# A scan with an FFN woven in: loads of delta moved up in the queue's list, and ScalarE's takes from the shared PSUM bank moved behind tanh

## The reference, cut to what matters

```python
x = _layernorm(x + _L0_attn_ref(x, ...))
x = _layernorm(x + _L0_ffn_ref(x, W1, W2, W3))      # silu(x W1) * (x W3), fwht, W2
x = _layernorm(x + _L1_attn_ref(x, W_bc, W_dt, b_dt, A_log, D_param))
x = _layernorm(x + _L1_ffn_ref(x, w_gate_up, w_down))
...
# _L1_attn_ref: 2 sequences of 1024 tokens, 512 channels, 32 states each
delta = softplus(dt_r @ W_dt + b_dt)                # dt_r, Bm, Cm are parts of x @ W_bc
def step(h, inp):                                   # over the time of one sequence
    dA  = exp(delta_t[:, :, None] * A[None])
    dBu = (delta_t * u_t)[:, :, None] * B_t[:, None, :]
    h   = dA * h + dBu
    y_t = einsum('bdn,bn->bd', h, C_t)
```

## Time and profile before

| | |
|---|---|
| median of three runs | 1904.08 us (1896.26 to 1905.1) |
| profiled execution | 1897.86 us, span 1896.0 us |
| TensorE busy | 1761.6 us (93%), 9472 matmuls |
| VectorE busy | 1328.4 us (70%), 1532 instructions |
| GpSimd busy | 1285.5 us (68%) |
| ScalarE busy | 983.3 us (52%) |
| loads of delta | 256, 512 KB each, median 5.5 us to landing |

### The profile page before, as it was taken

How to read it: one execution, slowest core, us unless ns; L and a number is a source line. 1 busy time by engine, 2 the same in 40 slices (tenths; PEclk the granted TensorE clock), 3 DMA queues, 4 the chain that set the end, 5 groups by cost and what they waited for, 6 DMA issues and landing times. The chain is left out here.

```text
span 1896.0 us, 27444 instructions
## 1 busy us (share of the span) xinstructions
PE 1761.6 (93%) x9472; PEld 1152.8 (61%) x9472; DVE 1328.4 (70%) x1532; ACT 983.3 (52%) x1671; POOL 1285.5 (68%) x992
## 2 busy tenths in 40 slices
PE   7898998898998999989899899988999999999998
PEld 5566666576755565555555555555556555667886
DVE  2525344332259999799897999889999999994222
ACT  5344343566465656645566556556555655543212
POOL 4533445255449998688887998888889898883111
PEclk9999999999999999999999999999999999999999
DMA  7442332587668887678676887777678777874652
GB/s 244 129 144 74 123 105 97 184 304 269 242 215 277 290 297 254 211 265 289 226 252 230 291 283 257 230 243 248 230 264 280 253 258 260 278 265 157 209 191 97
DMA packets 159226, 427.32 MB, mean 225 GB/s; under 512 B 30992, under 2 KB 54096, under 8 KB 158704
## 3 DMA queue, kind: packets, MB, share of 16 engines
q1 hardware_dynamic: 159088, 425.57, 66.6%
HBM read 356.30 MB, written 69.21 MB: 224 GB/s over the span
## 5 line engine op out<-in xcount | busy, mean ns | idle before, releaser
L1630 ACT ACTIVATE decay<-delta_on_states,a_neg 128x512 f32<-128x512 f32 x512 | 354.2, 693 | 361.8 <-DVE h_states L1770 336.2
L1865 POOL TENSOR_TENSOR q_or_raw_or_h_times_c<-h_states,c_rep 128x512 f32<-128x512 f32 x293 | 382.0, 1316 | 63.9 <-PE scan_y L1464 34.3
L1865 POOL TENSOR_TENSOR h_times_c_rest<-h_states,c_rep 128x512 f32<-128x512 f32 x219 | 283.8, 1306 | 43.7 <-DVE h_states L1770 22.0
L1831 POOL TENSOR_TENSOR h_lo<-v_or_silu_in_h_lo,h_hi 128x512 fp32r<-128x512 f32 x128 | 167.9, 1312 | 205.4 <-ACT h_hi L1537 204.8
L1770 DVE TENSOR_TENSOR_SCAN h_states<-decay,h_last,d_b 128x512 f32<-128x512 f32 x192 | 243.2, 1281 | 9.2 <-ACT decay L1630 4.4
L1770 DVE TENSOR_TENSOR_SCAN h_states<-decay,d_b 128x512 f32<-128x512 f32 x192 | 231.4, 1216 | 14.8 <-ACT decay L1630 10.5
L111 PE MATMUL y_or_aux<-h_hi,w 128*128 128x512 f32 x468 | 208.2, 445 | 8.5 <-POOL h_lo L1831 5.2
L1455 PE MATMUL du_spread<-stack,selectors 96*128 96x512 bf16 x512 | 159.0, 389 | 48.8 <-DVE d_b L1739 22.5
L1696 DVE SCALAR_TENSOR_TENSOR v_or_silu_in_h_lo<-v_or_silu_in_h_lo,gate_or_scores 128x512 f32<-128x512 f32 x127 | 86.5, 681 | 147.7 <-ACT v_or_silu_in_h_lo L1533 147.3
L112 PE MATMUL y_or_aux<-h_lo,w 128*128 128x512 f32 x468 | 185.1, 395 | 0.0
L113 PE MATMUL y_or_aux<-h_hi,w 128*128 128x512 f32 x468 | 184.3, 394 | 0.0
(11 more groups left out here) (252 smaller groups left out, 4187.9 us busy)
## 6 DMA issues: line engine op xcount, KB each, us to landing
delta_on_states<-delta SPq DMA_DIRECT2D x256, 512.0 KB, 5.5
w<-w_split SPq DMA_DIRECT2D x112, 512.0 KB, 4.2
attn_w_hi_or_x_hi_w<-w_split SPq DMA_DIRECT2D x112, 512.0 KB, 4.1
attn_w_lo_or_x_lo_w<-w_split SPq DMA_DIRECT2D x112, 512.0 KB, 4.2
w_split<-w_presplit_hi_lo SPq DMA_DIRECT2D x32, 512.0 KB, 3.3
w_presplit_hi_lo<-in_w13b SPq DMA_DIRECT2D x32, 256.0 KB, 3.7
w_split<-attn_w_hi_or_x_hi_w SPq DMA_DIRECT2D x8, 1024.0 KB, 6.4
w_split<-attn_w_lo_or_x_lo_w SPq DMA_DIRECT2D x8, 1024.0 KB, 7.0
```

The lines of the kernel that those rows point to most:

```text
L1630: act.activation(da[:, s % ND], dring[:, s % NR], ACT.Exp, scale=a[:, column(s):column(s) + 1]).then_inc(s_da, 1)
L1831: pool.tensor_tensor(hl[:, idx % RH], sg[:, idx % RH], hh[:, idx % RH].bitcast(F32), ALU.subtract).then_inc(s_hl, 1)
L1865: pool.tensor_tensor(hc[s % NC_], hs[:, s % NH], crep[:, tile_of(s // SPO) % 2], ALU.mult).then_inc(s_hc, 1)
```

## The change

Three edits. `delta_load` stands first in SyncE's tick of an even step, for the pair s+6, where it stood late in the tick of the odd step behind it. `dt_take` stands one tick later for the tiles prepared in the scan (the matmul stays), and the last two tiles' `states` move by one tick, matmul and copy. In the scan's ticks the whole list of ScalarE's takes (`take_bank`) stands behind `tanh`, `h_high` and `copy_input`, not ahead of them. Ahead of the scan the order is as it was.

```diff
--- before.py
+++ after.py
@@ -955,7 +955,7 @@
 SPLIT_TICK = (FIRST_TICK, 84, 163, 282, 374, 469, 556, 665)
 RANK_TICK = (106, 215, 312, 408)
 DT_TICK = ((107, 109, 111, 112), (216, 221, 225, 229), (317, 321, 325, 329), (413, 417, 421, 425))
-STATES_TICK = ((114, 115), (233, 235), (330, 332), (426, 428))
+STATES_TICK = ((114, 115), (233, 235), (331, 333), (427, 429))
 SOFT_TICK = (((108, (0,)), (114, (1, 2, 3))), ((230, (0, 1, 2, 3)),), ((330, (0, 1, 2, 3)),), ((426, (0, 1, 2, 3)),))
 PARTS_TICK = ((109, 123, 131, 139), (231, 239, 247, 255), (332, 340, 348, 356), (428, 435, 442, 449))
 PARTS_STEPS = (0, 1, 2, 1, 3, 5, 6, 8)
@@ -997,6 +997,7 @@
 RANK_AT = at_tick(RANK_TICK)
 RANK_COPY_AT = {tick + (t > 0): t for t, tick in enumerate(RANK_TICK)}
 DT_AT = at_tick_by_m(DT_TICK)
+DT_TAKE_AT = {tick + (key[0] > 0): key for tick, key in DT_AT.items()}
 STATES_AT = at_tick_by_m(STATES_TICK)
 SIZE_AT, INPUT_AT, HIGH_AT, DELTA_STORE_AT, REST_AT, MID_AT, LOW_AT, PARTS_STORE_AT = (
     at_tick_by_m(PARTS_TICK, step) for step in range(8))
@@ -1290,6 +1291,8 @@
                 constants()
                 for tick in range(FIRST_TICK, LAST_TICK):
                     s = step_at(tick)
+                    if s >= 0 and s % 2 == 0 and s + NR < STEPS:
+                        delta_load((s + NR) // 2)
                     if tick in RAW13_AT:
                         raw13_load(RAW13_AT[tick])
                     if tick in W13_STORE_AT:
@@ -1315,8 +1318,6 @@
                     if s == -4:
                         for pair in range(NR // 2):
                             delta_load(pair)
-                    if s >= 0 and s % 2 == 1 and s + NR - 1 < STEPS:
-                        delta_load((s + NR - 1) // 2)
                     o, step = divmod(s, SPO)
                     if s >= 0 and step == 20 and 2 <= o + 1 < NO:
                         stack_load(o + 1)
@@ -1641,15 +1642,7 @@
                     act.wait_ge(s_hs, s + 2)
                     act.copy(last[:, column(s):column(s) + 2], hs[:, s % NH:s % NH + 2, TT - 1]).then_inc(s_ca, 1)
 
-                for tick in range(FIRST_TICK, LAST_TICK):
-                    s = step_at(tick)
-                    if tick in W13_HIGH_AT:
-                        w13_high(W13_HIGH_AT[tick])
-                    if s == -1:
-                        copy_input(0)
-                        copy_input(1)
-                    if 0 <= s + 1 < STEPS:
-                        decay(s + 1)
+                def take_bank(tick):
                     if tick in MEAN_PARTS_AT:
                         mean_parts(MEAN_PARTS_AT[tick])
                     if tick in MEAN_AT:
@@ -1662,14 +1655,28 @@
                         rank_copy(RANK_COPY_AT[tick])
                     if tick in STATES_AT:
                         states_copy(*STATES_AT[tick])
-                    if tick in DT_AT:
-                        dt_take(*DT_AT[tick])
+                    if tick in DT_TAKE_AT:
+                        dt_take(*DT_TAKE_AT[tick])
+
+                for tick in range(FIRST_TICK, LAST_TICK):
+                    s = step_at(tick)
+                    if tick in W13_HIGH_AT:
+                        w13_high(W13_HIGH_AT[tick])
+                    if s == -1:
+                        copy_input(0)
+                        copy_input(1)
+                    if 0 <= s + 1 < STEPS:
+                        decay(s + 1)
+                    if tick < SCAN_TICK:
+                        take_bank(tick)
                     if tick in TANH_AT and TANH_AT[tick]:
                         tanh(TANH_AT[tick])
                     if tick in H_SPLIT_AT:
                         h_high(H_SPLIT_AT[tick])
                     if 0 <= s < STEPS and s % JB == 1 and s // JB + 2 < STEPS // JB:
                         copy_input(s // JB + 2)
+                    if tick >= SCAN_TICK:
+                        take_bank(tick)
                     if s >= 4 and s % 2 == 0 and s - 4 < STEPS and keeps(s - 4):
                         carry(s - 4)
                     for e, k in SQUARE_AT.get(tick, ()):
```

## The result

The changed kernel takes 1905.15 us in the median of 21 runs, the kernel before 1897.43 us on the same chip: ratio 1.0049, 95% interval 1.0037 to 1.0061. It is slower, by about 9.3 us (0.0049 x 1897). The whole interval lies over 1, where I had forecast no change; the difference is just inside my bound of 0.5%, and 1905.15 is inside the range, but the sum of the parts gave +1.8 us, and the difference is five times that. That 1905.15 is close to the 1905.9 of the sum on the median is luck: the first three runs put the kernel before 6.7 us too high (1904.08 against 1897.43), and the sum put the change 7.5 us too low. The profiled execution took 1903.71 us, its core's span 1901.8 us, 5.8 more than before.

What follows compares the result with a forecast made beforehand. TensorE and VectorE were taken as both near full in the scan, with TensorE setting the pace at the moved dt takes. Terms -4.3 + 1.0 + 0.5 + 6.7 - 1.1 - 1.0 = +1.8 us; forecast 1903 us, range 1889 to 1914.

Steps and rivals of the forecast that it cites:

- the sum of the parts: All terms of the change: -4.3 + 1.0 + 0.5 + 6.7 - 1.1 - 1.0 = +1.8 us.
- What bounds the kernel: Scan: TensorE and VectorE both near full, about a tick apart; VectorE's idle 83 us is all order can win.
- Rival A: Scan: VectorE sets the pace, so what `tanh` wins behind a take stays won, 13.7 us; 1887.5 us, chance 0.18.
- Part 1's gain: Earlier delta loads end late landings, chiefly the wait at tick 136 (3.3 us): -4.3 us in all.
- The other 1.0 us: Elsewhere, three VectorE waits for `tanh` behind a wait for delta, largest 0.43 us: taken as 1.0 us gain.
- Rival C: Delta loads still go out only when `decay` frees the slots; the takes alone count: 1907 us, chance 0.15.
- What part 1 pushes back: SyncE's list behind the early load: stack loads later, +1.0 us, and parts stores later, +0.5 us.
- Rival B: Stack loads late in most of the 14 blocks at 1.2 us each: 1919 us, chance 0.14.
- Part 2's stall: `down` waits for the later `dt_take` at ticks 226, 322, 418: 3 x 2.15 - 0.38 + 0.65 = +6.7 us.
- The 0.65 us: Takes of ticks 221, 317 and 413, behind only `decay`, hold TensorE: 0.65 us in all.
- The gain at tick 216: `decay` goes two microseconds earlier, ending the dt matmul's 1.11 us wait for VectorE's add: -1.1 us.
- `copy_input`'s: `copy_input` ahead of the logarithm frees three spreads that waited up to 0.65 us: -1.0 us, at most 2.

Runs made afterwards that it cites:

- q4: q1 with the takes behind `tanh` and those of dt a tick later, delta loads as before: 1891.56 us, 0.9974.
- q6: q4 with `dt_take` ahead of `tanh` again, still a tick later: 1881.33 us, 0.9923.
- e1: The kernel before with the first edit alone, `delta_load` first in SyncE's tick of even steps: 1902.92 us, 1.0027.
- q2: The changed kernel with size and input products reading decays in PSUM, as in q1: 1897.26 us, 1.0010.
- q3: e1 with size and input products reading decays in PSUM, as in q1: 1892.88 us, 0.9986.
- q5: q3 with the delta loads in the same even tick but last in its list: 1880.92 us, 0.9920.
- q1: The kernel before with the scan's size and input products reading decays in PSUM (softplus and step input not computed): 1884.13 us, 0.9932.
- e3: The kernel before with only the takes of means, variances and states behind `tanh`, `h_high` and `copy_input`: 1895.53 us, 0.9989.
- m1 to m3: Three small kernels: a VectorE sum beside GpSimd trains, varying train length (first), start (second), operand mix and scan ahead (third): no sum over 1.76 us.

## Why the prediction was wrong

**What bounds the kernel**: nothing in the runs speaks against it. Rival A (what `tanh` wins behind a take stays won) is refuted: in the changed kernel VectorE's wait for `tanh` fell by 7.6 us and the kernel got slower, and q4 waits 3.9 us less for `tanh` than q6 (24.9 against 28.8) and takes 9.7 us more.

**Part 1's gain** was right: 3.3 us forecast for the wait of tick 136; at ticks 137 and 138 the changed kernel and e1 gain 3.8 us, q2 and q3 4.6. The other 1.0 us wasn't seen by itself. Rival C (the loads don't go earlier) is refuted by the same.

**"What part 1 pushes back" is the step that failed.** I took +1.0 for stack loads and +0.5 for parts stores, 1.5 us. q3 against q5, which differ in nothing but the place in the list, measure 12.5 us without stands; in the true kernel e1 lies 5 us over before where the sum had -2.8, so the term there is about 9 (5.1 + 4.3 from my own gain). I priced each store by its own issue of 0.5 us and looked at whether `decay` was done at the tight places. Three things were left out. The load's 512 KB go ahead of the store and of the stack, so the landing, not only the issue, comes later (4.70 to 5.85 us for the store of tick 131, 5.87 to 9.17 for the stack of tick 240). The stack load waits for the store's landing at the head of SyncE's list, with the next loads of delta behind it: a store that is 1 us late makes a stack 2.2 us late and a `decay` 1.46 us late. And where `decay` isn't done, the store stands behind the load's wait for it, and at tick 138 it goes out 4.8 us later. Rival B had one of these, the stack, but not its shape: it is not most of the 14 blocks at 1.2 us, but two in q3 (3.97 and 1.1 us) and one at 1.8 us in the changed kernel, and the rest of the loss goes by the delta loads and the casts, which wait 30.0 us for stores in q3 and 22.8 in q5.

On the landings I had set the trace against the fit of the Trainium skill ("DMA: Bandwidth & Descriptors", Anatomy of one DMA). The section gives it for transfers that GpSimd issues, and all of these are SyncE's. The shortest landing of a 512 KB load here, 3.8 us, is over its 3.2 as well.

**Part 2's stall** was right in mechanism and places. In size it comes out by luck: 3 x 2.15 - 0.38 = 6.1 us, and q4 against q6 shows 1.3 + 3.2 + 1.6 = 6.1, but the waits are 1.39, 1.84 and 1.84 us, 5.1 in all, and the second costs 3.2 because the clock falls behind it, which was in no term. (The four parts of 2.15 add up to 2.17.) The 0.65 us for the takes without a `tanh` ahead doesn't show: TensorE waits for no take there. The rule of the Trainium skill ("PSUM — Partial Sum Buffer", Engine vs sequencer instructions) that matmuls start and complete in program order agrees with the trace: behind the `down` that waits until 1002.04 VectorE idles 2.69 us for the spread of 1005.43, and in q6 the same product has no wait. Missing was tick 330 and its like: a take behind `tanh` that waits for its gate starts `soft` 1.16 us later. I wrote that `soft` hangs on the last dt matmul and then costed it at nothing; it hangs on the take. With two such places 6.1 + 2.3 = 8.4 us, beside 9.7 measured. In the true kernel the takes lost 3.4 us of a forecast 4.6.

**The gain at tick 216** of 1.1 us is there, 1.5 us at tick 218. For it and `copy_input`'s together I had 2.1, and q6 is 1.7 us under q1; for `copy_input`'s alone 1.0, and e3 is 2.1 us under before. Neither is more than its uncertainty, so only the trace's 1.5 us is shown.

**VectorE's stands** were in no term. The size products take 26.2 us in the trace before, 1745 ns each where 0.69 would do; I passed over that group because the change didn't touch it. Together with `step_input`'s share it is 12.9 us of the kernel, and in the traces of before and after, where a stand falls moves the steps by as much as any part of the change.

**The clock** was in no term either, and no run holds it fixed. In the profiled executions the granted clock is 0.50 for 31 us of the scan before and for 41 us after; over all executions its mean is 0.986 to 0.987 before and 0.984 after. Among executions of one kernel the time moves with it (the changed kernel: 1901.84 us at 0.989, 1913.57 us at 0.981), over all of them by about 0.5 us for each us of clock lost. By this, an estimate, the clock carries 2 to 3 of the 9.3 us, and 3 of the 12.5 between q3 and q5. Part of it is the change's own doing, as behind the stall of 1.84 us.

## What to carry to other kernels

A load that is moved to the front of an in-order queue takes its wait and its bytes with it: price what stands behind it by landings, above all a transfer whose landing the queue itself waits for. Try the place behind the stores first: here it kept the gain, and the place in front cost 12.5 us. A take that sits ahead of an operation that waits anyway cost nothing here; put behind it, it held its bank's next user and everything that hangs on it. A wait's length isn't its cost: compare the starts of what waits, and against how late the kernel already is. And when two versions differ by half a per cent, take the chance meetings of VectorE and GpSimd out of both, and look at the granted clock, before believing a ledger of waits.

## What the runs showed of the hardware

A VectorE product or sum of two 128x512 SBUF operands takes 0.69 us alone and 0.67 to 1.76 us beside GpSimd's products, by when it starts and whatever the length of the train; with one operand in PSUM 0.687. The Trainium skill ("SBUF — State Buffer", Who interferes with whom) says that the two engines share one pair of ports, an exclusive lock, that a VectorE instruction with two SBUF inputs contends with a GpSimd instruction that reads SBUF, and that one with at most one SBUF input, outside its two-port modes, doesn't: m1 to m3 agree. But in the scan the size product took 3.8 to 6.1 us none to three times in 15, through two to four whole GpSimd instructions, and when it was freed, the next product stood 3.0 to 5.6 us. What makes these long is open: in the small kernels train length, moment, semaphores, operand mix and a scan ahead didn't bring one about; beside DMA traffic, ScalarE and TensorE it wasn't tried. Each kernel has one trace, so how much the stands change from one execution to the next isn't known.

Behind 1.84 us in which TensorE stood, its granted clock fell to 0.50 for over 3 us and matmuls started 0.43 us apart in place of 0.23; behind another wait of 1.84 us (`down` at 1217.69) it stayed at 1.00.
